# A graph and attention block on one core: the order of norm, one-hots, counts, turns of x and basis groups at its start

## What is computed

```
xn = _layernorm(x)
# a relational graph layer, twice; two relations r
w   = einsum('rb,bio->rio', att, basis)      # 2 x 512 x 512 out of 30 bases
gate = sigmoid(x_j @ gate_w[r]);  msg = gate * x_j @ w[r]      # by edge type
out = segment_sum(msg, row, 625) + x @ root + bias
x = x + graph(xn) + attention(xn)
```

## Time and profile before

| | us |
|---|---|
| median of 3 runs | 979.17 (977.83, 979.17, 983.41) |
| time of the profiled execution | 982.54 |
| its span, first to last instruction | 980.4 |
| PE busy in the span | 920.4 |
| DVE busy | 621.8 |
| ACT busy | 400.0 |
| mean granted clock of PE | 0.982 |

### The profile page before, as it was taken

One profiled execution on the slowest core, in us unless ns is written; L12 is line 12 of the kernel. 1 busy time (PEld: TensorE's weight loads), 2 busy tenths in 40 slices (PEclk: granted clock), 3 DMA queues, 4 the chain that ended last, 5 costly groups with the idle time before them and its releaser, 6 DMA issues. The chain is left out here.

```text
span 980.4 us, 12366 instructions
## 1 busy us (share of the span) xinstructions
PE 920.4 (94%) x4576; PEld 609.5 (62%) x4576; DVE 621.8 (63%) x1272; ACT 400.0 (41%) x670; POOL 111.8 (11%) x98
## 2 busy tenths in 40 slices
PE   3889899999999999999998999999999999999997
PEld 1445554674544674488756556989997644545885
DVE  6997988877976842353117652788786524658861
ACT  4877874311113111021113332577875534424540
POOL 0000000000300231100011000253430000023200
PEclk9998999999999999989999999999999999999899
DMA  8979769578712350064976004122004000230001
GB/s 301 337 276 375 262 257 386 205 259 276 240 46 92 133 197 1 0 236 155 320 264 220 3 1 129 49 86 77 11 1 168 5 1 13 80 86 0 1 1 53
DMA packets 63886, 137.31 MB, mean 140 GB/s; under 512 B 6143, under 2 KB 20099, under 8 KB 63810
## 3 DMA queue, kind: packets, MB, share of 16 engines
q1 hardware_dynamic: 62690, 134.95, 39.3%
q0 software_dynamic: 1120, 1.29, 0.5%
HBM read 132.84 MB, written 3.38 MB: 139 GB/s over the span
## 5 line engine op out<-in xcount | busy, mean ns | idle before, releaser
L415 PE MATMUL PS<-AR 128*125 128x512 f32 (+9 forms) x1394 | 394.2, 440 | 9.7 <-DVE AR L1227 1.8
L415 PEld LDWEIGHTS PS<-AR 128*128 128x128 f32 (+3 forms) x1394 | 212.4, 194 | 170.2 <-issue 162.0
L1984 ACT ACTIVATE AR<-PS 128x500 f32<-128x500 f32 (+6 forms) x73 | 41.9, 578 | 153.8 <-PE PS L415 75.6
L1987 ACT ACTIVATE AR<-iota,AR 125x625 f16<-125x625 f16 x119 | 85.9, 812 | 24.6 <-PE PS L502 24.6
L1397 DVE SCALAR_TENSOR_TENSOR AR<-spare,cst,AR 128x512 f32<-128x512 f32 x96 | 69.7, 778 | 13.0 <-DMA spare<-in_rest 12.9
L500 PE MATMUL PS<-AR 125*125 125x512 f16 (+9 forms) x425 | 62.7, 305 | 8.1 <-issue 6.8
L1287 DVE TENSOR_SCALAR AR<-iota,AR 125x625 f16<-125x625 f16 x165 | 60.5, 443 | 12.4 <-PE PS L502 12.3
L500 PEld LDWEIGHTS PS<-AR 125*125 125x125 f16 x425 | 46.7, 143 | 27.7 <-issue 18.8
L2480 POOL TENSOR_TENSOR whl<-AR,whh 128x512 fp32r<-128x512 f32 x32 | 47.7, 1512 | 89.9 <-ACT whh L1984 89.9
L447 PE MATMUL PS<-AR 128*32 128x512 f32 x276 | 41.9, 617 | 16.8 <-DMA AR<-in_basis 15.0
L1832 DVE TENSOR_TENSOR HMl<-AR,HMh 128x626 fp32r<-128x626 f32 x64 | 51.3, 840 | 4.6 <-ACT HMh L1984 4.6
(11 more groups left out here) (325 smaller groups left out, 1507.1 us busy)
## 6 DMA issues: line engine op xcount, KB each, us to landing
AR<-in_basis SPq DMA_DIRECT2D x46, 768.0 KB, 8.8
spare<-in_rest SPq DMA_DIRECT2D x48, 512.0 KB, 4.3
AR<-in_L_ffn_W SPq DMA_DIRECT2D x20, 1024.0 KB, 7.6
spare<-in_basis SPq DMA_DIRECT2D x18, 768.0 KB, 8.5
AR<-in_L_gnn_Wh SPq DMA_DIRECT2D x8, 512.0 KB, 4.1
AR<-in_L_gnn_Wh SPq DMA_DIRECT2D x16, 256.0 KB, 4.8
AR<-in_L_mix_W_qkv SPq DMA_DIRECT2D x4, 768.0 KB, 8.3
AR<-in_L_gnn_root SPq DMA_DIRECT2D x2, 1024.0 KB, 6.5
```

The costliest lines, as they stand in the source:

```text
L415: ins = te.matmul(o, l, r, start=start and i == 0, stop=stop and i == len(pairs) - 1)
L1984: return se.activation(o, i, ACT.Copy, scale=scale)
L1987: return se.activation(o, i, f, bias=bias, scale=scale)
```

## The change

`AFTER` gets group 0 behind segment 0. A dictionary `TURN` puts the turn of chunk c behind segment 2 + 2c. PE starts with the counts. A turn now writes into CB, the one bank that the groups use; so it waits for the result of the last group to be read, and the next group waits for the turned chunk to be copied out. On DVE `ends(0)` stands ahead of the reduction of the counts, `ends(1)` behind it, then the statistics of all five chunks; the five scalings come in iteration 0 behind `ends(2)`, and gate products move by one iteration. On ACT `ends(1)` follows `ends(0)` directly; the roots come in iteration 0 behind `ends(2)`. No arithmetic is added or removed.

```
-AFTER = [g // 2 + 1 if g % 2 else None for g in range(NS - 2)] + [12, 13]
+AFTER = [0] + [g // 2 + 1 if g % 2 else None for g in range(1, NS - 2)] + [12, 13]
+TURN = {2 + 2 * c: c for c in range(5)}
...
-            pe.wait_ge(am_ready, 6)
-            combos(0)
...
-            pe.wait_ge(d_cst, 16)
-            for c in range(NT):
+            def turn0(c, groups):
+                pe.wait_ge(d_cst, 16)
                 pe.wait_ge(xn_ready, LN_X + c + 1)
-                turn(("xt", 0, c), c, XN, 4, "dve" if c % 2 else "act")
+                pe.wait_ge(w_ready, groups)
+                u = psum.take(("xt", 0, c), "dve" if c % 2 else "act", slot=3)
+                slot(u)
+                for k in range(4):
+                    ins = te.transpose(CB[:, k * P:(k + 1) * P], XN[0:P, c, k * 128:(k + 1) * 128], ident[0:P, 0:P])
+                ins.then_inc(u.sem, 1)
...
-                if AFTER[g]:
+                if AFTER[g] is not None:
+                    if g == 0:
+                        pe.wait_ge(am_ready, 6)
+                    if g - 1 in TURN:
+                        read(psum["xt", 0, TURN[g - 1]])
                     combos(AFTER[g])
+                if g in TURN:
+                    turn0(TURN[g], sum(n is not None for n in AFTER[:g]))
...
-            dv.wait_ge(d_x, 16)
-            for c in range(NT):
-                ln_stats(X, 512, c)
-                if c:
-                    ln_scale(X, c - 1, LN_X + c)
-            ln_scale(X, NT - 1, LN_X + NT)
...
+            dv.wait_ge(d_iota, 16)
+            ends(0)
             for i, (b0, b1) in enumerate(((0, 3), (3, 5))):
...
-            for c in (1, 3):
-                turned(("xt", 0, c), c, 4, XT)
...
-            dv.wait_ge(d_iota, 16)
-            ends(0)
             ends(1)
+            dv.wait_ge(d_x, 16)
+            for c in range(NT):
+                ln_stats(X, 512, c)
...
                 dv.wait_ge(flush_done, NT * f + b + 1)
+                dv.wait_ge(gl_ready, NT)
...
-                if g and AFTER[g - 1] and AFTER[g - 1] % 2:
+                if g and AFTER[g - 1] is not None and AFTER[g - 1] % 2:
                     combo_in(AFTER[g - 1])
+                if TURN.get(g - 1, 0) % 2:
+                    turned0(TURN[g - 1])
...
-                if g < NT:
+                if g == 0:
+                    for c in range(NT):
+                        ln_scale(X, c, LN_X + c + 1)
+                if 0 < g <= NT:
                     dv.wait_ge(d_gw0, 16)
-                    dv.wait_ge(xn_ready, LN_X + g + 1)
-                    gate_rows(0, g, lambda r: sums[0][:, 0, 1:513])
+                    dv.wait_ge(xn_ready, LN_X + g)
+                    gate_rows(0, g - 1, lambda r: sums[0][:, 0, 1:513])
...
             ends(0)
+            ends(1)
             ac.wait_ge(pool_const, 1)
-            for c in range(NT):
-                ln_root(c, LN_X + c + 1)
...
-            combo_out(0)
-            for c in (0, 2, 4):
-                turned(("xt", 0, c), c, 4, XT)
-            ends(1)
...
-                if AFTER[g] and AFTER[g] % 2 == 0:
+                if g == 0:
+                    for c in range(NT):
+                        ln_root(c, LN_X + c + 1)
+                if AFTER[g] is not None and AFTER[g] % 2 == 0:
                     combo_out(AFTER[g])
+                if TURN.get(g, 1) % 2 == 0:
+                    turned0(TURN[g])
```

More of the change, by code:

```diff
@@ L1258, in gate_rows, with turned0 @@
                 ins.then_inc(gl_ready, 1)
-            dv.wait_ge(d_x, 16)
-            for c in range(NT):
-                ln_stats(X, 512, c)
-                if c:
-                    ln_scale(X, c - 1, LN_X + c)
-            ln_scale(X, NT - 1, LN_X + NT)
[L1267 to L1278, removed]
-            for c in (1, 3):
-                turned(("xt", 0, c), c, 4, XT)
+            def turned0(c):
+                full(("xt", 0, c))
+                ve.tensor_copy(XT[:, :, cols(c)], CB[:, 0:4 * P].rearrange("p (k n) -> p k n", k=4)).then_inc(dve_read, 1)
             def ends(g):
@@ L1304, in _ @@
             ends(0)
+            for i, (b0, b1) in enumerate(((0, 3), (3, 5))):
+                k = full(("cnt", i))
+                ve.tensor_reduce(flags[0:1, b0:b1, :],
+                                 sl(k, 0, (b1 - b0) * EP, 1).rearrange("p (b g t) -> p b g t", g=NS, t=7),
+                                 AX_X, ALU.add).then_inc(dve_read, 1)
+            read(psum["cnt", 1])
+            for b in range(NT):
+                t = step(ve.tensor_scalar(flags[0:1, b, :], flags[0:1, b, :], 0.0, float(1 << b), ALU.is_gt, ALU.mult))
+            dv.wait_ge(*t)
+            t = step(ve.tensor_reduce(met[:, :], flags[0:1, :, :].rearrange("p b g -> p g b"), AX_X, ALU.add))
+            dv.wait_ge(*t)
+            ve.tensor_copy(imet[:, :], met[:, :]).then_inc(flags_ready, 1)
             ends(1)
+            dv.wait_ge(d_x, 16)
+            for c in range(NT):
+                ln_stats(X, 512, c)
             for z, o in enumerate((OFF0, OFF1)):
@@ L2012, in _, with turned0 @@
             ends(0)
+            ends(1)
             ac.wait_ge(pool_const, 1)
-            for c in range(NT):
-                ln_root(c, LN_X + c + 1)
+            def turned0(c):
+                full(("xt", 0, c))
+                copy(XT[:, :, cols(c)], CB[:, 0:4 * P].rearrange("p (k n) -> p k n", k=4)).then_inc(act_read, 1)
             def combo_out(k):
```

## The result

The changed kernel took 984.33 us (median of 17 runs), the kernel before 980.92 (17 runs beside them): a ratio of 1.0035, 95% interval 1.0018 to 1.0052. That is the case within 0.5%, which had the largest chance, but on the other side of zero from the forecast, and 1.1 us above the end of the range. One of the 17 executions took 1857 us and is left out of the ratio.

The account below looks back on a forecast made before the run. PE bounds nearly the whole span, DVE the segment loop at the start. The time gained there shrinks to 1.3 us at the second pass, less 0.1 for hand-offs: 979.17 - 1.2 = 978.0 us, range 973.3 to 983.2.

Parts of the forecast that it names:

- the case within 0.5%: Whole time: a change of under 4.9 us, which a measurement can't tell from no change; chance 0.72.
- the slow value: Segment 0 on PE: 3.8 us as before, against 2.1 for other segments, so it ends at 19.6.
- rival 5: ACT's table loads in the loop: a drain holds up the first copy by 2.1 us, time 980.1; chance 0.02.
- The toll of CB: Turns and copies in the groups' one bank: 1.1 us a turn on average, leaving 1.3 us gained at the second pass.
- Rival 2: Groups wait for turned chunks: 3.3 us slower, 982.5, if a turn costs over 1.3 us on average; chance 0.11.
- the lead: Segment loop: `ends(2)` starts 11.2 us earlier; 5.7 remain at segment 4's end and 1.3 at the second pass.
- Rival 1: Copies and turns fit into PE's waits: 4.9 us at segment 6 reach the end, 974.3; chance 0.16.
- The step that failed: Group 1 at the loop's start: load 7, issued at about 20.2, lands at 29, and the group ends at 29.9.
- The bound that failed: Load 7's landing ahead of group 1: 4 us shorter or longer, of which about 1 stays behind the flush.
- Rival 3: Second pass and segment 12: no half-clock stretch in the new timing, 4.2 us more come back, 973.8; chance 0.07.
- Rival 4: First pass, at full clock before, gets a half-clock stretch too: 4.2 us more, 982.2; chance 0.04.

Follow-up runs that it names:

- the run where they came in time at full clock: Changed kernel with the gate weights loaded behind basis load 7 and the turns behind segments 12 to 20: 987.25 us, ratio 1.0090.
- the first experiment: Changed kernel with the gate weights loaded behind basis load 7 instead of ahead of load 5, gate products one iteration later: 981.44 us, ratio 1.0001.

## Why the prediction missed: the landing of load 7

**What held.** The loop starts at 13.96 (forecast "about 14"). `ends(2)` is on DVE at 20.89 ("near 20"). Segment 0 ran at the slow value, its windows at 0.52 of the clock, and ended at 20.8 (19.6). ACT's two table loads have no drain behind them, so the price by the Trainium skill (ScalarE: Activation LUTs, What ACT_TABLE_LOAD costs), some 1.38 us for each switch, is not borne out: 0.02 us of idle time, as before; rival 5 is out. PE waits for copies ahead of groups 3 and 4, as named, 2.81 and 1.84 us (forecast: the longest about 1.5).

**The toll of CB.** From the end of segment 2 to the second pass the forecast had 53.0 us (32.0 to 85.0) and the trace has 52.6 (37.7 to 90.25). The sum turn by turn held to 0.4 us, but its parts moved and cancelled, which was luck: group 3's wait was longer, group 2 waited too, group 6 didn't. The kernel before took 47.1 us for this stretch (39.2 to 86.29), so against it the five turns cost 5.4, 1.1 each, as summed. Rival 2 had the right sign and nearly the right size, 3.3 us slower, and its sign, a second pass "after 87", came. But it decides "when a turn costs over 1.3 us on average", counted against the kernel before, and that was 1.1. The 1.4 to 1.5 of the experiments are counted against kernels with no turns in the stretch, which run it in 45 us. What lacked was the lead, 5.7 us of it at group 1. Rival 1, with a second pass before 82, is out.

**The step that failed** is "At a median of 8.8 to landing it is there at 29. Group 1 ends at 29.9". Load 7 landed at 34.4, group 1 ended at 35.6: 5.7 late, and the second pass is 90.25 - 85.0 = 5.3 late. In the terms of the sum 1.9 us are the issue (22.07 instead of 20.2) and 3.5 the landing (12.3 us instead of 8.8), but the issue is no cause, as the table of landings shows: behind the broadcast load 7 lands at 32 to 36 us whenever it is issued, and without it at 27 to 29. What the prediction had wrong is the price of the load. In the trace of the kernel before this very load took 16.9 us and landed at 34.2, and loads 5 and 6, which the prediction didn't count and whose issue the change doesn't move, landed at 30.4 and 32.3. Group 1 of the kernel before ran right behind its loads and ended at 37.1. The last load is followed by some 0.9 us of work, so work moved ahead of it could win some 2 us there, not 7. Of group 1's 5.7 us, 4.4 are the loads (35.6 against 31.2 in the run where they came in time at full clock), and the other 1.3 are mostly ACT's chain, which ended at 28.0 instead of 26.9. A median over 46 loads was taken as the price of one that stands behind a broadcast in full queues; the profile of before had the low rate on show as well, 238 to 248 GB/s from 20 to 26 us, with the DMA share at 1.0.

**The bound that failed** is "the landing may be 4 us shorter or longer, of which about 1 stays behind the flush". The landing was 5.4 longer, beyond that bound, and nearly all of it stayed: 5.3 of the 5.7 us at group 1 stand at the second pass, and the first experiment moved group 1's end by 2.5 and both later passes by 2.5. The delay of 5.3 us at the second pass, put on the forecast, gives 978.0 + 5.3 = 983.3, at the end of the range and within 1.1 us of the 984.3 measured. A late landing passed on whole should have been a rival with a chance of its own; it was a bound of 1 us.

**The clock.** Rival 3's mechanism came about in the profiled execution: the second pass ran at full clock and won 4.2 us, which is why the two profiled executions agree. But it doesn't show in the medians: the recorded mean clock of all runs is 0.983 for the changed kernel and 0.984 to 0.985 for the one before, so the spell was not saved on the whole. Rival 4's happened with other kernels (52 to 67 us with the gates and the turns moved, 88 to 101 where ACT copies first). Where a spell falls depends on the timing in a way that these runs don't resolve; that the time goes with the clock over the runs is seen in the table: before ranges from 984.1 at 0.981 to 977.9 at 0.988.

**What stays open**: what decides the place of a low-clock spell; what makes the landing of the same load differ by 4 us between executions; and why turns moved ten segments later give a time some 1.6 us lower at an equal clock, with the last segment equally late. That the broadcast's low rate is what delays the loads behind it was shown only by moving it; another form of that load wasn't tried.

## What to carry to other kernels

Work moved ahead makes only what has its inputs earlier; follow the load that the next consumer needs, issue and landing, before the lead is put into the sum, and price its landing by what that very load took in the trace rather than by a median over the kernel. Where a consumer runs right behind its loads, it shows no wait, and yet it can't come earlier. Count a delay as passed on whole unless a wait in the chain behind it is shown to take it in. Where two profiled executions agree and medians don't, compare windows for the granted clock first, and runs at equal clock next.

## What was unexpected of the hardware

- A broadcast load can hold the DMA engines full at 0.6 to 0.7 of the rate: 230 to 277 GB/s with a share of about 1.0 against some 400 right after it, for about 8 us. Load 5, right behind it, took 17.5 us, and 9.4 where the broadcast stood later; load 7 landed at 31.8 to 35.8 behind it, whether issued at 17 or at 22 us, and at 27.4 to 28.9 ahead of it.
- The granted clock went to 0.50, the 1.2 GHz level, in stretches in which PE was busy without a gap (2.00 of 2.00 us), on one-row openings and zero matmuls in a pass, and at group 1 behind 2.3 us of waiting. The record can also miss a spell: 1.00 from 14 to 20 us, with the matmuls of segment 0 as slow as at 0.50 (3.98 us for 14). With the work that keeps PE busy in the passes the recorded mean clock was 0.985 instead of 0.979, and it cost more time than that gave.
- A bank passed to and fro between PE and a copying engine took 1.4 us a round at full clock, of which the turn is 0.6 and the copy 0.6, and 1.8 to 2.0 at half, with a turn of 1.1.
